# Three edits in a twelve-layer kernel: scaled queries made by ScalarE, the context's part moved into the first pass, biases as two exact parts

## The reference, cut to what matters

```python
x = x + _L0_attn_ref(_layernorm(x), ...)               # layer 0: bidirectional state space layer
x = x + _L0_xattn_ref(ctx_1024, _layernorm(x), ...)    # layer 1: latent attention over the context
x = x + _L0_ffn_ref(_layernorm(x), ...)                # layer 2: experts
x = x + _L1_attn_ref(_layernorm(x), w_qkv, w_pre, w_post, w_out, b_out)   # layer 3: head mixing
...
# inside layer 3, 16 heads of 16 numbers
q, k = apply_rope(q), apply_rope(k)
dots = einsum('bhid,bhjd->bhij', q, k) * scale
dots = einsum('bhij,gh->bgij', dots, w_pre)
attn = softmax(dots)
attn = einsum('bhij,gh->bgij', attn, w_post)
out = einsum('bhij,bhjd->bhid', attn, v)
return out @ w_out.T + b_out
```

## Time and profile before

| | |
|---|---|
| time, median of 3 | 4476.31 us (4470.59 to 4476.92) |
| time of the profiled execution | 4478.14 us |
| its span, first to last instruction | 4476.3 us |
| mean granted TensorE clock | 0.92 |
| busy: PE, DVE, ACT, POOL | 86%, 71%, 48%, 31% of the span |
| span of layer 0's loop | from 79 to 1035 us |
| layer 3 | from 2068 to 2650 us |

### The profile page before, as it was taken

One profiled execution on the slowest core, in us unless ns is written; L12 is line 12 of the kernel. 1 busy time (PEld: TensorE's weight loads), 2 busy tenths in 40 slices (PEclk: granted clock), 3 DMA queues, 4 the chain that ended last, 5 costly groups with the idle time before them and its releaser, 6 DMA issues.

```text
span 4476.3 us, 57633 instructions
## 1 busy us (share of the span) xinstructions
PE 3847.8 (86%) x20186; PEld 2643.3 (59%) x20186; DVE 3182.3 (71%) x7349; ACT 2163.2 (48%) x5232; POOL 1392.8 (31%) x963
## 2 busy tenths in 40 slices
PE   5778788768999989998999998788797979778997
PEld 2323233325666669986888885455565558336776
DVE  5989999995666667666888976566576754543768
ACT  5666667564544532222333348367576622432334
POOL 3989898981000000001222223553310000100004
PEclk8889998889999999999999998699998989878998
DMA  3434444442000000000000010000000010000000
GB/s 108 139 130 150 132 149 139 136 151 82 1 1 1 1 22 29 20 10 13 1 1 1 1 39 1 13 1 1 12 2 2 1 38 1 39 0 19 1 1 19
DMA packets 83426, 180.16 MB, mean 40 GB/s; under 512 B 9051, under 2 KB 14275, under 8 KB 80579
## 3 DMA queue, kind: packets, MB, share of 16 engines
q1 hardware_dynamic: 83139, 176.49, 11.8%
HBM read 173.84 MB, written 2.62 MB: 39 GB/s over the span
## 4 chain that ended last, share of the span: by engine, by line
PE 36%; DVE 12%; ACT 4%; issue 2%; POOL 1%; DMA 0%; DVEq 0%; ACTq 0%; POOLq 0%
PE PS L210 29%; PE PS L217 5%; DVE qg L2156 1%; DVE stat L287 1%; DVE p L3466 1%; PE PS L3187 1%; DVE hl L2387 1%; DVE qg L2151 1%; ACT p L2683 1%; ACT p L3479 1%; DVE XNr L324 1%; DVE W L2392 0%; DVE wc L3391 0%; DVE p L3631 0%; POOL far L3594 0%
## 5 line engine op out<-in xcount | busy, mean ns | idle before, releaser
L210 PE MATMUL PS<-db,cst 128*128 128x512 f32 x1024 | 544.8, 680 | 159.1 <-DVE db L1205 159.0
L1200 DVE TENSOR_TENSOR_SCAN db<-PS,db 128x512 f32<-128x512 f32 x512 | 591.3, 1204 | 46.0 <-ACT PS L1165 34.2
L210 PEld LDWEIGHTS PS<-db,cst 128*128 128x128 f32 x1024 | 208.0, 214 | 468.8 <-DVE db L1205 241.2
L217 PE MATMUL PS<-cst,p 128*128 128x128 f32 (+1 forms) x2880 | 394.3, 283 | 55.1 <-DVE pt L3151 23.5
L217 PEld LDWEIGHTS PS<-cst,p 128*128 128x128 f32 (+1 forms) x2880 | 335.6, 147 | 114.5 <-issue 36.7
L210 PE MATMUL PS<-xnT,W 128*128 128x256 f32 (+2 forms) x1072 | 338.9, 464 | 17.4 <-ACT pt L2709 7.5
L1146 POOL TENSOR_TENSOR db<-du,b 128x1024 f32<-128x1024 f32 x128 | 307.9, 2433 | 12.9 <-PE PS L210 11.4
L1146 POOL TENSOR_TENSOR db<-W,b 128x1024 f32<-128x1024 f32 x128 | 310.3, 2451 | 1.8 <-PE PS L210 1.4
L2105 ACT ACTIVATE p<-PS,sm 128x256 f32<-128x256 f32 x256 | 119.0, 470 | 376.8 <-DVE sm L2162 376.8
L210 PEld LDWEIGHTS PS<-xnT,W 128*128 128x128 f32 (+1 forms) x1072 | 214.4, 204 | 141.1 <-issue 95.0
L1972 POOL TENSOR_TENSOR rb<-rb,tb 128x512 f32<-128x512 f32 x32 | 41.1, 1285 | 798.8 <-DVE tb L1967 798.8
(11 more groups left out here) (445 smaller groups left out, 8615.0 us busy)
## 6 DMA issues: line engine op xcount, KB each, us to landing
b<-bc_rows SPq DMA_DIRECT2D x256, 256.0 KB, 3.6
c<-bc_rows SPq DMA_DIRECT2D x256, 256.0 KB, 3.7
W<-in_we SPq DMA_DIRECT2D x9, 1024.0 KB, 4.8
W<-in_w SPq DMA_DIRECT2D x1, 4224.0 KB, 13.1
W<-in_w SPq DMA_DIRECT2D x1, 4122.5 KB, 14.0
W<-in_w SPq DMA_DIRECT2D x1, 4100.0 KB, 12.2
W<-in_w SPq DMA_DIRECT2D x1, 2313.0 KB, 10.0
X<-in_x SPq DMA_DIRECT2D x4, 512.0 KB, 16.7
```

The costliest lines, as they stand in the source:

```text
L210: ins = T.matmul(out, l, r, start=first and i == 0, stop=last and i == len(pairs) - 1)
L217: ins = T.transpose(bank[0:m, c:c + r], s, ident[0:r, 0:r])
L1200: V.tensor_tensor_scan(db[:, f, r], self.ring.PS[:, self.BANKS[x % 3], r], db[:, f, r], 0.0, ALU.mult, ALU.add).then_inc(self.sc.sem, 1)
```

## The change

- **State space layer.** The context's work is cut into parts (raw transposes with the statistics and normalised copy; normalised transposes) and put at three places of the first pass: after SILU (CTX), after LN (CTX + 1, PE and ACT only) and after MAX (CTX + 2, DVE only). Its raw and normalised copies lie in the gate and y tiles; the first gate copy waits for its end. The small weights of layer 0 move ahead, and the first load takes them too (2212 columns instead of 2048). Rows of C have four buffers instead of three. In the first pass POOL makes the second half of du after the first three products instead of before them.
- **Head mixing.** ACT makes the high part of q (`act_high`), two units ahead of DVE; DVE makes only the rest.
- **Biases.** In layers 3, 4, 5, 7 and 10 the bias lies in rows 0 and 32 of its block. DVE rounds both to fp32r and puts in row 32 the difference from the bias; the bias product is one fp32r product over 33 rows. The biases of layer 9 stay as they were.

```diff
@@ -24,9 +24,8 @@
 
 
 SPEC = {
-    0: [("Win", 2048), ("Wdt0", 512), ("Wdt1", 512), ("Wout", 1024), ("Wxd0", 384), ("Wxd1", 384),
-        ("conv", 16), ("bconv", 4), ("D0", 4), ("D1", 4), ("bdt0", 4), ("bdt1", 4),
-        ("A0", 64), ("A1", 64)],
+    0: [("Win", 2048), ("conv", 16), ("bconv", 4), ("D0", 4), ("D1", 4), ("bdt0", 4), ("bdt1", 4), ("A0", 64),
+        ("A1", 64), ("Wxd0", 384), ("Wdt0", 512), ("Wxd1", 384), ("Wdt1", 512), ("Wout", 1024)],
     1: [("Wq", 2048), ("Wkv", 4096), ("Wout", 2048), ("mg", 2), ("mb", 2), ("lg", 2), ("lb", 2)],
     2: [("rw", 16), ("rb", 1), ("b1", 36), ("b2", 256)],
     3: [("Wqk", 1024), ("Wv", 512), ("Wout", 512), ("wpre", 32), ("wpost", 256), ("bo", 256)],
@@ -492,10 +491,32 @@
     def pool(self, e):
         pass
 
+    def setup_bias(self, name, n):
+
+        E = self.E
+        o, w = offsets(SPEC[self.n])[0][name]
+        self.b_in = E.region(self.n)[0:33, o:o + n * w]
+        self.b_ones = E.tile(f"bias_ones{self.n}", P, FR)
+        self.b_parts = E.tile(f"bias_parts{self.n}", n * w, FR)
+        self.b_made = E.counted("dve_w", 1)
+
+    def dve_bias(self, e):
+        V = e.eng
+        e.wait_ge(*self.w_ready)
+        V.tensor_copy(self.b_ones[0:33, :], self.E.K("one", 33))
+        V.tensor_copy(self.b_parts[0:33, :], self.b_in).then_inc(e.own, e.up())
+        e.wait_ge(e.own, e.ups)
+        V.tensor_tensor(self.b_parts[32:33, :], self.b_in[32:33, :], self.b_parts[32:33, :],
+                        ALU.subtract).then_inc(self.b_made.sem, 1)
+
+    def bias_product(self, e, i, rows=P):
+        e.wait_ge(*self.b_made(1))
+        return [(self.b_ones[0:33, 0:rows], self.b_parts[0:33, i * D:(i + 1) * D])]
+
     def pe_to_x(self, e, t, parts, bias=None):
         bank = self.ring.take(e, ("x", self.n, t), self.x(t + 1))
         if bias is not None:
-            parts = parts + [(self.E.ones[0:1, :], bias)]
+            parts = parts + self.bias_product(e, bias)
         mm(e.eng, bank[:, 0:D], parts).then_inc(self.wo.sem, 1)
 
     def dve_to_x(self, e, t):
...
@@ -542,11 +567,11 @@
         for c in range(4):
             e.eng.dma_start(E.X[:, 4 * c:4 * c + 4, :], xv[:, 4 * c:4 * c + 4, :]).then_inc(self.x_sigs[c].sem, 16)
             if c == 0 and self.first:
-                e.eng.dma_start(E.region(0)[:, 0:2048], A["w0"][:, 0:2048]).then_inc(self.win.sem, 16)
+                e.eng.dma_start(E.region(0)[:, 0:E.small0], A["w0"][:, 0:E.small0]).then_inc(self.win.sem, 16)
             if c == 0 and self.context:
                 e.eng.dma_start(self.raw[0:S2], A["ctx"].rearrange("b s d -> s b d")).then_inc(self.ctx_in.sem, 16)
             if c == 0:
-                E.load_weights(e, LAYERS[0], 2048 if self.first else 0)
+                E.load_weights(e, LAYERS[0], E.small0 if self.first else 0)
 
     def parts(self, h):
         st = self.st[h][0:S2]
...
@@ -583,41 +624,40 @@
                 ins = V.tensor_scalar(self.nrm[0:S2, 4 * h + j, :], self.raw[0:S2, 4 * h + j, :], mv[:, j, 0:1],
                                       rs[:, j:j + 1], ALU.subtract, ALU.mult)
             ins.then_inc(self.xn.sem, 1)
-        for i, (src, dst, k, h) in enumerate(self.banks):
-            if i % 2:
-                e.wait_ge(*self.tp(i + 1))
-                V.tensor_copy(dst[:, k, 4 * h * S2:4 * (h + 1) * S2],
-                              self.ring.of(("ctx", i))[:, 0:4 * S2]).then_inc(self.cd.sem, 1)
 
     def act(self, e):
         e.wait_ge(*self.z(1))
         for s in range(32):
             self.nxt.act(e, s, self.nxt.early)
-        if self.context:
-            self.act_context(e)
-
-    def act_context(self, e):
+        if self.context and not self.first:
+            self.act_context(e, 0)
+            self.act_context(e, 1)
+
+    def act_context(self, e, norm):
         C = e.eng
-        for h in range(2):
+        for i, (src, dst, k, h) in enumerate(self.banks):
+            if i % 2 == 0 and src == norm:
+                e.wait_ge(*self.tp(i + 1))
+                C.activation(dst[:, k, 4 * h * S2:4 * (h + 1) * S2], self.ring.of(("ctx", i))[:, 0:4 * S2],
+                             ACT.Copy).then_inc(self.ca.sem, 1)
+        for h in range(2) if norm == 0 else ():
             mv, bs, sd, rs = self.parts(h)
             e.wait_ge(*self.stats(h + 1))
             C.activation(sd, mv[:, :, 1], ACT.Sqrt, bias=self.E.eps[0:S2]).then_inc(self.sd.sem, 1)
-        for i, (src, dst, k, h) in enumerate(self.banks):
-            if i % 2 == 0:
-                e.wait_ge(*self.tp(i + 1))
-                C.activation(dst[:, k, 4 * h * S2:4 * (h + 1) * S2], self.ring.of(("ctx", i))[:, 0:4 * S2],
-                             ACT.Copy).then_inc(self.ca.sem, 1)
 
     def pe(self, e):
         for s in range(32):
             self.nxt.pe(e, s, self.nxt.early)
-        if self.context:
-            self.pe_context(e)
-
-    def pe_context(self, e):
+        if self.context and not self.first:
+            self.pe_context(e, 0)
+            self.pe_context(e, 1)
+
+    def pe_context(self, e, norm):
         e.wait_ge(*self.c_in(1))
         e.wait_ge(*self.ctx_in(1))
         for i, (src, dst, k, h) in enumerate(self.banks):
+            if src != norm:
+                continue
             if src:
                 e.wait_ge(*self.xn(h + 1))
             a = self.nrm if src else self.raw
@@ -720,7 +760,7 @@
         self.delta.append(E.tile("delta1", 2048))
         self.du.append(E.tile("du1", 2048))
         self.db = [E.tile(f"db{i}", 1024) for i in range(6)]
-        self.c_ = [E.tile(f"c{i}", 512) for i in range(3)]
+        self.c_ = [E.tile(f"c{i}", 512) for i in range(4)]
         self.b_ = [E.tile(f"b{i}", 512) for i in range(3)]
         self.bc = E.nc.dram_tensor("bc_rows", (8, 32, 512), F32, kind="Internal").ap()
         self.dd = split(E.tile("dd", 512), 4)
...
@@ -764,6 +806,7 @@
             zero.update({self.WIN + f: 27 + 2 * f, self.UP + f: 28 + 2 * f, self.CONV + 2 * f: 35 + 3 * f,
                          self.CONV + 2 * f + 1: 36 + 3 * f, self.UA + f: 37 + 3 * f})
         zero[self.SILU] = 46
+        self.todo[2].append((self.READY, 0, self.DU + 1))
         zero.update({j: 47 + x for j, x in steps.items()})
         for c in range(4):
             for j, x in steps.items():
@@ -782,10 +825,10 @@
     READY, GATE, OUT, ADDX = 0, 1, 2, 3
     WIN, CONV, SILU, DT, DTA, WDT, ABS, EXP, LN, ONE, SUB, MAX, ADD, DU, ROWS = (
         0, 4, 12, 13, 15, 16, 20, 21, 22, 23, 25, 27, 29, 31, 33)
-    UP, UA, DLA = 34, 38, 42
+    UP, UA, DLA, CTX = 34, 38, 42, 46
     FIRST = (WIN + 2, UP + 2, WIN + 3, UP + 3, CONV + 4, CONV + 6, WIN, UP, WIN + 1, UP + 1, CONV, CONV + 1, UA, CONV + 2,
-             CONV + 3, UA + 1, SILU, DT, DT + 1, DTA, ROWS, WDT, DLA, WDT + 1, DLA + 1, WDT + 2, DLA + 2, WDT + 3, DLA + 3,
-             ABS, EXP, LN, MAX, MAX + 1, DU, DU + 1)
+             CONV + 3, UA + 1, SILU, CTX, DT, DT + 1, DTA, ROWS, WDT, DLA, WDT + 1, DLA + 1, WDT + 2, DLA + 2, WDT + 3,
+             DLA + 3, ABS, EXP, LN, CTX + 1, MAX, MAX + 1, CTX + 2, DU)
 
     def dl(self, k):
 
...
@@ -869,8 +912,8 @@
 
     def sp_c(self, e, i):
         c, p, d, k, s = self.of(i)
-        e.wait_ge(*self.c_used(i - 3))
-        e.eng.dma_start(self.c_[i % 3], self.bc[k, 16 + s].partition_broadcast(P)).then_inc(self.cd_[i % 3].sem, 16)
+        e.wait_ge(*self.c_used(i - 4))
+        e.eng.dma_start(self.c_[i % 4], self.bc[k, 16 + s].partition_broadcast(P)).then_inc(self.cd_[i % 4].sem, 16)
 
     def steps(self, e, norm, nxt, piece, one, two, three):
         for j in self.FIRST:
...
@@ -951,6 +994,9 @@
                 bank = ring.take(e, ("gate", k, f), self.gac(4 * k + f + 1))
                 mm(T, bank, [(self.Win[:, i, 512 + f * P:512 + (f + 1) * P],
                               self.E.xnT[:, i, k * 512:(k + 1) * 512]) for i in range(2)]).then_inc(self.gp.sem, 1)
+        elif j >= self.CTX:
+            if j < self.CTX + 2 and self.prev.context:
+                self.prev.pe_context(e, j - self.CTX)
         elif j < self.CONV:
             f = j
             self.inn.wait(e, c)
@@ -1004,6 +1050,8 @@
             f, r = divmod(j, 2)
             if r:
                 e.wait_ge(*self.yd(2 * k))
+                for token in self.E.ctx_ready if k == 0 else ():
+                    e.wait_ge(*token)
                 e.wait_ge(*self.gp(4 * k + f + 1))
                 C.activation(v4(self.G)[:, f, :], ring.of(("gate", k, f)), ACT.Copy).then_inc(self.gac.sem, 1)
             if j == 7:
...
@@ -1023,9 +1074,7 @@
             if c:
                 e.wait_ge(*self.sum_of(64 * (c - 1) + 32))
             else:
-                e.wait_ge(*self.w_ready)
-                for token in self.E.ctx_ready:
-                    e.wait_ge(*token)
+                e.wait_ge(*self.E.win_ready)
             e.wait_ge(*self.cv(4 * c + f - 1 if c else f + 1))
             C.activation(v4(self.u)[:, f, :], ring.of(("conv", c, f)), ACT.Identity,
```

(25 more changed lines are left out.)

105 lines of the change are left out of this document (68 added, 37 removed).

## The result

The changed kernel takes **4406.35 us** (4404.46 to 4408.78, 4 runs) against 4476.61 (4470.59 to 4478.18, 4 runs) for the kernel before on the same chip: ratio 0.9846, 95% interval 0.9829 to 0.9863, so 70 us faster. The profiled span went from 4476.3 to 4404.7.

What follows compares the result with a forecast made beforehand. The prediction took the bound to be twelve layers run one after another, each edit read in its own stretch. Terms -15.3, -23.8 and -19.0 sum to -58.1; 4478.1 - 58.1 - 1.8 gives 4418 us, range 4395 to 4445.

Steps and rivals of the forecast that it cites:

- A: State space layer: earlier start, reordered context and du work, and a fourth buffer for C, together -15.3 us.
- First product: Start of the state space layer: its first product comes at 13.9 instead of 23.89, -10.0 us.
- DT behind the fourth group: State space layer's start: the fourth group of raw context transposes waits for a bank, so DT starts later, +1.1 us.
- The du order: Layer 0's first pass: POOL's products start earlier, so DVE's first scan comes at 77.2 instead of 79.25, -2.0 us.
- near 68: Sign to look for in layer 0: DVE's first scan comes near 68 us.
- nothing, at worst +2: Layer 0: PE waits for a bank DVE frees before pass 1's DT; expected to cost nothing, at worst 2 us.
- C buffer: State space loop: C's loads issued one step earlier remove five DVE waits for ACT, -4.4 us, bounds 0 and -10.
- B: Layer 3's head mixing: 1.6 us off each of 13 PE waits, plus 3.0 in the first three units, -23.8 us.
- C: Biases: 0.32 us saved on each of 88 products, weighted by share on the path, less 1.0 for parts, -19.0 us.
- the share on the path: Bias savings counted fully in layers 3 and 10 (10.2), two thirds in 7 (3.4), half in 4 and 5 (6.4).
- rival 1: Low parts still held by POOL and 33-row products drain the array like 1-row ones: 4442 us, chance 0.24.
- Rivals 2 to 4: 2: switching costs vanish, 4396, chance 0.10; 3: stalls move, 4470 to 4476, 0.03; 4: ACT bounds layer 3, 4570, 0.02.

Runs made afterwards that it cites:

- du_first: The changed kernel with GpSimd making both halves of du before its first products again, as before the change: 4405.34 us, ratio 0.9842 to the kernel before.
- three_c: The changed kernel with three buffers for rows of C instead of four: 4412.28 us, ratio 0.9861 to the kernel before.
- no_b: The changed kernel with the head mixing part undone, VectorE making q's high and low parts in the same unit again: 4434.51 us.
- no_c: The changed kernel with the old bias product (two fp32 records over one row) in all 88 places: 4430.06 us.
- fp32_128: The changed kernel with its 88 bias products in fp32 again, two records each, but over all 128 rows: 4403.86 us.
- rows128: The changed kernel with its 88 bias products over all 128 rows instead of 33, the added rows zero: 4381.13 us.

## Why the prediction was right, and where not

**A, forecast -15.3.** Layer 0 shortened by 13.8. *First product* -10.0: it came 9.8 earlier, ACT's copy of DT 10.08, and chunk 0's first write of X 10.1 (362.43 to 352.35). The step holds. *DT behind the fourth group* +1.1: DT starts at 35.27, 0.7 late against 44.58 - 10.0, by the wait for ACT L641 that the text named, but its product takes 5.31 instead of 6.09, so the term comes to nothing. *The du order* -2.0: **this step failed as worked out.** It had DVE's two operations at 1.2 each and the first scan at 77.2 on the old axis; measured from ACT's copy of DT, the scan came 1.7 late instead of 2.0 early, at 70.86, where the forecast's sign was "near 68". POOL's products, brought forward to 61.48, lie beside DVE's L1144 and L1146, which take 2.0 more each. The prediction quoted the rule for the low parts and did not ask where else POOL was moved beside DVE. For the same reason the step "nothing, at worst +2" went the bad way: DVE frees the bank for pass 1's DT product at 68.9 (65.3 in `du_first`), and ACT waits 2.24 for that product (not at all in `du_first`). The Trainium skill (SBUF — State Buffer, "SBUF: two separate sides") says that a DVE operation with two SBUF inputs and a GpSimd operation that reads SBUF shut each other out for a whole instruction; 3.25 against 1.23 beside three products of 3.06 agrees. Thirty microseconds on, the order was 1.07 ahead, and `du_first` shows no difference in time. *C buffer* -4.4: `three_c` gives 5.9, and 3.7 by the loops' own gain; right, and the five waits gone through one by one were the right ones. ACT's wait for C, which was to be gone, is still there, but 17.8 in 22 places instead of 88.6 in 51. That A as a whole is within 1.5 is in part luck: two of its terms, +1.1 and -2.0, came to nothing and nearly cancel.

**B, forecast -23.8.** `no_b` gives -28.2 for the kernel and -30.7 for the layer. The mechanism is right in all its steps: the 13 waits behind rope tiles are gone, the first three units keep 3.4 of 6.7, the first low part runs at once (0.48) and the second waits for POOL (1.49), 1.88 the pair, ACT's copies are hidden (0.49 to 0.56 each, less than the 0.587 of the nearest row, and 0.40 from start to start). What was mis-sized is the price of a wait: only its length was counted. PE's idle time fell by 22.6, near the 23.8, the 4.7 that it now waits for p taken in; but it was also busy 8.4 less, up to 6.8 of it by four spells at the lower clock that are gone.

**C, forecast -19.0.** `no_c` gives -23.7. The price of a product, 0.32, was right to the hundredth. That a product over 33 rows still pays the visit was right too: the four records ahead stay at 0.96. The Trainium skill (TensorEngine Tiling (Array Packing), "Key Properties") says that a change of the array's tiling mode drains it. 0.96 with 1 and with 33 rows against 0.68 with 128 fits that; the 0.87 of `fp32_128`, where all products have 128 rows, is not covered by it. What failed is **the share on the path**: layer 3 gives 5.1 (forecast 5.1), 7 4.6 (3.4), 10 4.1 (5.1), but layer 4 alone 14.6 to 16.5, where 4 and 5 together were put at 6.4. "ACT and DVE are as often the last" does not hold in layer 4, where PE's busy time and the layer grow alike, by 14.7 and 14.6, and with the lower clock it comes to twice the products' price. DVE's parts, put at +1.0 in layer 10, take 0.9 there (4017.42 to 4018.28) while DVE has nothing else to do, and nothing waits for them.

**Where the miss lies.** To the end of layer 10 the profiled executions differ by 72.0, the forecast had 58.1: layer 0 -1.5, layer 3 +2.4, layers 4 and 5 +12.9, layer 7 +1.8, layer 10 -1.1, the unchanged layers 8 and 9 -1.7, the parts +1.0. Layer 5's 5.2 are not its biases': with the old product back (`no_c`) it takes 321.0, less than the 323.2 of the changed kernel and than the 328.4 of before. Its granted clock was 0.85 before, 0.86 after and 0.89 in `no_c`; what sets it there is open.

**Rivals.** Of rival 1 both parts are to be seen: the pair is held by POOL, and 33 rows don't spare the visit. Neither has its price: the pair is held by one operation and ends as PE comes, and the slot shrank by 0.32 all the same. Rivals 2 to 4 did not come; 4396 would have needed the visits gone, as in `rows128`.
